# Local attention of a 12-layer transformer stack: probabilities divided before they are turned, outputs produced turned

## The reference, cut to what matters

```python
def local_attention(q, k, v):               # 16 heads, 64 features a head, windows of 32 tokens
    ...                                     # each window looks at the one before it and at itself
    sim = jnp.einsum('bhwie,bhwje->bhwij', bq, bk2) * QK_SCALE
    sim = jnp.where(mask, -jnp.finfo(sim.dtype).max, sim)
    attn = jax.nn.softmax(sim, -1)
    out = jnp.einsum('bhwij,bhwje->bhwie', attn, bv2)
    return out.reshape(b, h, n, d)

def attn_layer(x, Wqkv, qs, ksc, Wo):
    ...                                     # q, k, v from x; q and k to length 1, scaled, rotated
    out = local_attention(q, k, v)
    out = out.transpose(0, 2, 1, 3).reshape(b, n, INNER)
    return out @ Wo
```

## Time and profile before

| what | us |
|---|---|
| median of 3 runs | 4365.75 |
| lowest and highest run | 4363.63 and 4371.05 |
| span of the profiled execution | 4366.1 |
| busy TensorE, matmuls (weight loads) | 3908.6 (2744.4) |
| busy GpSimd | 3002.4 |
| busy VectorE | 2756.9 |
| busy ScalarE | 2682.7 |

### The profile page before, as it was taken

The page is one execution under the profiler, slowest core; times in us unless marked ns, Lnnn a source line. Parts: engine busy times, 40 slices in busy tenths (PEclk is TensorE's granted clock), DMA queues, the critical chain, the costliest instruction groups (busy, mean ns, idle before and its releaser), DMA issues.

```text
span 4366.1 us, 169503 instructions
## 1 busy us (share of the span) xinstructions
PE 3908.6 (90%) x69444; PEld 2744.4 (63%) x69444; DVE 2756.9 (63%) x4939; ACT 2682.7 (61%) x5560; POOL 3002.4 (69%) x1858
## 2 busy tenths in 40 slices
PE   7889999999999999977999999999999998265975
PEld 5556666676666766744766666666666665153645
DVE  5566666676766666734667676677676764623751
ACT  5657666676666767644676666767666675133752
POOL 0088888888888888814988888888888884611011
PEclk9999999999999999979999999999999998577987
DMA  2033433434334344311344343443433432031004
GB/s 68 2 86 90 112 97 95 110 93 107 97 95 104 96 105 102 93 46 42 96 102 104 92 111 93 103 108 92 108 98 96 108 92 55 0 104 27 2 13 127
DMA packets 349837, 367.90 MB, mean 84 GB/s; under 512 B 58738, under 2 KB 285299, under 8 KB 348787
## 3 DMA queue, kind: packets, MB, share of 16 engines
q1 hardware_dynamic: 338834, 348.59, 31.4%
q0 software_dynamic: 2048, 4.20, 0.3%
q10 hardware_dynamic: 8160, 3.93, 0.3%
HBM read 246.79 MB, written 109.71 MB: 82 GB/s over the span
## 4 chain that ended last, share of the span: by engine, by line
PE 38%; DVE 4%; ACT 4%; issue 3%; POOL 2%; DMA 1%; DVEq 0%; POOLq 0%; ACTq 0%
PE banks L328 6%; PE banks L356 4%; PE banks L369 4%; PE banks L416 3%; PE banks L460 3%; PE banks L312 2%; PE banks L295 2%; PE banks L401 2%; PE banks L454 1%; PE banks L386 1%; PE banks L1382 1%; ACT arena L996 1%; PE banks L1402 1%; DVE arena L619 1%; PE banks L923 1%
## 5 line engine op out<-in xcount | busy, mean ns | idle before, releaser
L690 POOL TENSOR_TENSOR arena<-arena 128x512 f32<-128x512 f32 x768 | 959.6, 1270 | 414.6 <-DVE arena L619 235.2
L695 POOL TENSOR_TENSOR arena<-arena 128x1024 f32<-128x1024 f32 x384 | 906.0, 2359 | 30.1
L692 POOL TENSOR_TENSOR arena<-arena 128x1024 f32<-128x1024 f32 x384 | 907.5, 2363 | 0.0
L619 DVE SCALAR_TENSOR_TENSOR arena<-arena,banks 128x512 f32<-128x512 f32 x768 | 493.5, 684 | 503.8 <-ACT arena L502 500.9
L328 PE MATMUL banks<-w_qk,arena 128*128 128x512 f32 x1536 | 734.5, 601 | 16.0 <-DVE arena L719 10.6
L470 ACT COPY arena<-banks 128x512 f32<-128x512 f32 x384 | 224.3, 584 | 656.8 <-PE banks L416 656.7
L612 DVE TENSOR_REDUCE arena<-arena 128x8 f32<-128x512 f32 x768 | 494.0, 679 | 86.1 <-ACT arena L486 84.2
L486 ACT ACTIVATE arena<-banks 128x512 f32<-128x512 f32 x768 | 441.3, 593 | 62.5 <-PE banks L328 50.5
L416 PE MATMUL banks<-ident,arena 128*128 128x128 f32 x3072 | 425.3, 282 | 28.6 <-POOL arena L695 20.5
L328 PEld LDWEIGHTS banks<-w_qk,arena 128*128 128x128 f32 x1536 | 276.4, 193 | 271.4 <-issue 271.4
L586 DVE TENSOR_REDUCE arena<-banks 128x8 f32<-128x512 f32 x384 | 264.0, 687 | 212.5 <-PE banks L312 212.1
(11 more groups left out here) (217 smaller groups left out, 6519.4 us busy)
## 6 DMA issues: line engine op xcount, KB each, us to landing
v_rows<-arena SPq DMA_DIRECT2D x1536, 64.0 KB
arena<-v_rows SPq DMA_DIRECT2D x768, 128.0 KB
arena<-v_rows SPq DMA_DIRECT2D x768, 112.0 KB
arena<-in_moe_w SPq DMA_DIRECT2D x30, 515.5 KB, 3.8
w_qk<-in_stack_qk SPq DMA_DIRECT2D x48, 256.0 KB, 3.0
w_v<-in_stack_v SPq DMA_DIRECT2D x48, 128.0 KB, 3.3
w_o<-in_stack_o SPq DMA_DIRECT2D x12, 512.0 KB, 3.9
w_w<-in_stack_w SPq DMA_DIRECT2D x12, 341.0 KB, 3.1
```

Source lines behind the costliest of these rows:

```text
L619: last = nc.vector.scalar_tensor_tensor(qn[:, :, tile], rn, 1e12, bank(M, tile).rearrange("p (h q d) -> p h q d", h=GH, q=2), ALU.min, ALU ...
L690: nc.gpsimd.tensor_tensor(f.sined[:, :, :, half, :], x[:, :, :, 1 - half, :], sines[:, :, mine].unsqueeze(1).to_broadcast([D, GH, 4, DH // ...
L692: nc.gpsimd.tensor_tensor(rot, x.rearrange("p h t a d -> p h t (a d)"), cosines.unsqueeze(1).to_broadcast([D, GH, 4, DH]), ALU.mult).then_ ...
L695: nc.gpsimd.tensor_tensor(rot, rot, f.sined.rearrange("p h t a d -> p h t (a d)"), ALU.add).then_inc(S.rotated, 1)
```

## The change

VectorE multiplies the probabilities `p` (128 by 512, in SBUF) by the reciprocal of their sums in place, right behind the reciprocal. TensorE turns the probabilities when that is done (`normed`) instead of when the exponential is done. In the output products the operands swap places: the weights are the 64 by 64 values of a window, the moving operand 32 columns of turned probabilities, and a product is 64 features by 32 tokens. With that the outputs need neither the multiplication of line 596 nor the turn of line 386; ScalarE copies them from the banks into `ot` directly, and the rows of the output weights are laid out to match. The outputs now use columns 0 to 255 of banks 4 and 5, as the scores do: they wait until the scores of this step have been shifted into `zs`, and the next scores wait until they have been copied. Their place in TensorE's order moves from behind the scores to behind the projection of queries and keys. On ScalarE their copy stands ahead of the copy of the values in all steps. VectorE no longer waits for outputs before the maximum. The buffer `o` and the signal `outs_turned` go.

```diff
 def pe_stack_step(M, st):
...
         st.wait(S.shifted, u)
-
-        st.wait(S.normed, u - 1)
+        st.wait(S.outs_taken, u - 1)
...
-    if st.on(4):
-        u = s - 4
-        st.wait(S.probs_taken, u + 1)
-        pe.wait_ge(S.v_loaded, st.n64 + 64 * (u + 1))
-        st.wait(S.normed, u)
-        pe.sem_inc(M.s.pe_waited)
-        for hp in range(2):
-            for win in range(NW):
-                c = 32 * (win % 4)
-                o = T + (win // 4 * 2 + hp) * DH
-                for par in range(2):
-                    r = slice(64 * par, 64 * par + 64)
-                    last = pe.matmul(bank(M, 4 + par)[c:c + 32, o:o + DH], f.pt[r, win // 4, hp, c:c + 32],
-                                     f.vb[r, u % 2, win, hp, :], start=True, stop=True)
-        last.then_inc(S.outs, 1)
...
-    if s % G == 3:
-
-
-        pe_stack_outs_turned(M, st)
-        pe_stack_probs_turned(M, st)
-        pe_stack_values(M, st)
-    else:
-        pe_stack_values(M, st)
+    pe_stack_outs(M, st)
+    pe_stack_values(M, st)
+    if s % G != 3:
         pe_stack_hidden(M, st, 1)
-        pe_stack_probs_turned(M, st)
-        pe_stack_outs_turned(M, st)
+    pe_stack_probs_turned(M, st)
...
+def pe_stack_outs(M, st):
+
+
+    pe, s, S, f = st.eng, st.s, M.st, stack_buffers(M)
+    if st.on(4):
+        u = s - 4
+        st.wait(S.probs_taken, u + 1)
+        pe.wait_ge(S.v_loaded, st.n64 + 64 * (u + 1))
+
+        if st.on(3):
+            st.wait(S.shifted, u + 2)
+        st.wait(S.outs_taken, u)
+        pe.sem_inc(M.s.pe_waited)
+        for win in range(NW):
+            c = 32 * (win % 4)
+            for hp in range(2):
+                for par in range(2):
+                    r = slice(64 * par, 64 * par + 64)
+                    last = pe.matmul(bank(M, 4 + par)[64 * hp:64 * hp + 64, 32 * win:32 * win + 32],
+                                     f.vb[r, u % 2, win, hp, :], f.pt[r, win // 4, hp, c:c + 32],
+                                     start=True, stop=True)
+        last.then_inc(S.outs, 1)
...
 def pe_stack_probs_turned(M, st):
...
-        st.wait(S.probs, u + 1)
+        st.wait(S.normed, u + 1)
...
 def pe_stack_heads(M, st, qk):
...
-        st.wait(S.outs_taken, u - 2)
+        st.wait(S.heads_taken, u)
...
 def act_stack_step(M, st):
...
-    if s % G == 3:
-        act_stack_outs(M, st)
-        act_stack_probs(M, st)
-        act_stack_values(M, st)
-    else:
-        act_stack_values(M, st)
+    act_stack_outs(M, st)
+    act_stack_values(M, st)
+    if s % G != 3:
         act_stack_hidden(M, st, 1)
-        act_stack_probs(M, st)
+    act_stack_probs(M, st)
...
     if s % G == 3:
         act_stack_hidden(M, st, 1)
-    else:
-        act_stack_outs(M, st)
     act_stack_hidden(M, st, 2)
...
 def act_stack_outs(M, st):
...
-        st.wait(S.outs_turned, u + 1)
+        st.wait(S.outs, u + 1)
...
-        nc.scalar.copy(stack_hidden(M).ot[:, u % G].rearrange("p h t -> p (h t)"), bank(M, 3)).then_inc(S.outs_taken, 1)
+        nc.scalar.copy(stack_hidden(M).ot[:, u % G], M.ps[:, 4:6, 0:T]).then_inc(S.outs_taken, 1)
...
 def dve_stack_step(M, st):
...
-        st.wait(S.outs, u)
...
-    if st.on(4):
-        u = s - 4
-        st.wait(S.outs, u + 1)
-        st.wait(S.inverted, u + 1)
-        st.wait(S.outs_turned, u)
-        nc.vector.tensor_tensor(f.o.rearrange("p (x b) d -> p x b d", b=2), two_banks(M, T, DH),
-                                f.inv.rearrange("p (x b) -> p x b", b=2).unsqueeze(3).to_broadcast([D, 4, 2, DH]),
-                                ALU.mult).then_inc(S.normed, 1)
-    if st.on(3):
-        u = s - 3
         st.wait(S.probs, u + 1)
         nc.vector.tensor_reduce(f.total, f.p, AX.X, ALU.add).then_inc(S.summed, 1)
         st.wait(S.summed, u + 1)
-        st.wait(S.normed, u)
         nc.vector.reciprocal(f.inv, f.total).then_inc(S.inverted, 1)
+        st.wait(S.inverted, u + 1)
+        nc.vector.tensor_tensor(f.p, f.p, f.inv.unsqueeze(2).to_broadcast([D, 8, KW]), ALU.mult).then_inc(S.normed, 1)
```

## The result

| | before | after |
|---|---|---|
| median | 4364.69 us (4363.57 to 4371.05, 4 runs) | 4773.74 us (4765.19 to 4780.62, 4 runs) |
| ratio | 1 | 1.0932, 95% interval 1.0914 to 1.0949 |
| span of the profiled execution | 4366.1 us | 4777.0 us |

The changed kernel is 9.3% slower, 409 us. The prediction said 4798 us and 4480 to 4900.

What follows compares the result with a forecast made beforehand. TensorE was taken as full (97% busy), closely followed by a loop through X, VectorE and GpSimd. Eight steps came to 76.5 against 67.5 us; 48 x 9.0 = 432 us on 4366.1 gave 4798 us, range 4480 to 4900.

Steps and rivals of the forecast that it cites:

- the rival with waits at any phase: Multiplication asks anywhere in GpSimd's time: mean wait 0.8 us instead of 2.1, total 4606; shares 0.70 with the main forecast.
- X: End of the scaling of queries and keys on VectorE, which frees VectorE, banks and GpSimd's rotation; 2.05 us into the next step.
- the hold: VectorE's multiplication, both operands in SBUF, waits for GpSimd's running instruction, up to 2.4 us, then takes 0.55; chance 0.70 (4600 to 4900).
- A bare step: Step without extras, from X to next X: multiplication ends at 5.75, turn starts at 5.8, plus 3.02, giving 8.82 us.
- The extras: Additions to eight steps of 8.82 us: feed-forward +0.69 and +0.74, last feed-forward matmul +1.0, steps behind a projection +1.6 and +1.9.
- by TensorE's own order: After the first step ending with the projection, TensorE's sequence alone sets 10.4 us from turn to turn, +1.6.
- its sister: The second step ending with the projection: VectorE asks at about X + 5.1 to 5.5, costing +1.5 or +2.4, taken as 1.9.
- The output block: The 64 output passes on TensorE, moved behind the projection of queries and keys: 1.1 us, ends 0.87 and 1.5.
- TensorE's own sum: TensorE's change per step from removed turn, new output passes and their old place: -0.1 us, ends -0.3 and +0.3.
- the rival of 5300: Weight loads queue on TensorE: output passes take 3.65 us, eight steps some 20 us longer; 0.07 together with half clock.
- The rival without a hold: Multiplication takes 0.69 us, loop 6.9, about 1 us extra in each of four steps: 71 per eight, 4534; chance 0.10.
- The rival of half clock: New waits of up to 2 us lower TensorE's granted clock, doubling matmuls at 1.2 GHz: above 4900; 0.07 together with queued loads.

## Why the prediction was right, step by step

- **The multiplication is held by GpSimd and ends 0.55 us behind it.** As forecast: mean 2.14 us in the range of 2 to 2.7, tail 0.55, most of them (286 of 384) in the third instruction, so the rival with waits at any phase (4606) did not come. In six of eight steps it asked at X + 2.98 to 3.74 (forecast 3.10 and 3.84) and ended at X + 5.43 to 5.84 (forecast 5.75). The kernel with the reciprocals in a bank shows that the hold is the cause.
- **GpSimd pays too.** "Some 0.5 longer" was too much: the fourth instruction took 2.69 instead of 2.36, 0.33 more. I had scaled from the earlier trace rows, where a multiplication of 1024 columns made it about 1 us longer.
- **A bare step of 8.82 us.** Steps 3, 6 and 7 took 8.54, 8.68 and 8.85 from turn to turn. Right.
- **The extras.** Forecast were 1.0 for the matmul ahead of the turn, 0.69 and 0.74 for two feed-forward instructions on VectorE, and 1.6 and 1.9 for the two steps behind a projection. Over 8.82, row 2 has 1.48, in which both the matmul (1.0) and the late X of step 1 (0.74) were to show; rows 4 and 0 have 2.21 each. The step that I let come "by TensorE's own order" (10.4) is held as well: its multiplication asks at X + 5.26 to 5.48 and falls into GpSimd's fourth instruction, ending at X + 8.02, near the other end (2.4) of what I weighed for its sister. So a wait that I had put down to TensorE alone was a hold. Against this, the feed-forward instruction of step 1 shows as 0.6 in its X, and that of step 5 as nothing (row 6 has 8.68); row 5 has 0.4 that I did not forecast, since the turn starts 0.55 behind the multiplication there. The errors cancelled: 76.4 against 76.5. The total is better than its terms, and that part is luck.
- **The output block.** Taken as 1.1 with ends at 0.87 and 1.5. It is 1.07 from start to start (1083.41 to 1084.48), and its neighbours grew: the projection ahead of it from 1.72 to 1.81 and the values behind it from 0.86 to 0.97 (medians over all steps), 1.27 in all. TensorE's own sum is thus about +0.1 a step instead of -0.1. Loads that queue, the rival of 5300, are refuted.
- **The order.** The prediction had X "3.02 us after the turn starts", by ScalarE's copy, and gave the hold the whole of the loss. Both stand in the same loop, and the experiments split them: without the hold 209 us go, without the hold and the tie 381. The rival without a hold was put at 4534 and the run gave 4564, 30 us off. As charged, four steps are longer there, s = 1, 3, 5 and 6, by 1.26, 0.89, 1.26 and 0.75 us; the other four are within 0.1 us of before, where I had taken off 0.1 us a step for TensorE.
- **TensorE's busy share.** Forecast down to about 80%, measured 90% in the stretch. Here my own sums did not agree: 65.5 us of busy time in 67.4 before, less 0.8, over 76.5 would have been 85%. For the other 5 points I have an argument only: a group's busy time includes its last matmul's tail, which lay over the next group before and now lies in a hole.
- **The clock.** TensorE's waits for the multiplication, up to 3.0 us long, left the granted clock at 0.99 in the stretch. The rival of half clock did not come.
- **The profiled execution.** Span 4777.0 less 4366.1 is 411 us; the loop's 430 less that leaves 19. Most of it is found at the starts of layers, for which the prediction took nothing off: the first step s = 7 after each of the ten starts inside the modules loses 1.4 to 3.2 us less than that step's median.

What is left of the change without hold and tie, the 56 us between the two kernels with the moved logarithm, is in the main a wait of TensorE for the feed-forward pieces. Their waits (idle before the matmuls: total, times, longest), with the new outputs:

```profile
PE banks L417 <- ACT ln_sq L528: 30.2, 48, 1.4
...
PE banks L445 <- ACT xc L542: 20.6, 52, 0.8
PE banks L445 <- DVE ln_sq L621: 13.4, 19, 1.6
```

and with the outputs of before:

```profile
PE banks L460 <- DVE ln_sq L651: 5.0, 4, 1.6
PE banks L460 <- ACT xc L563: 4.7, 6, 0.8
...
PE banks L432 <- ACT ln_sq L549: 2.9, 2, 1.4
```

64 us against 13: heads and pieces come 0.75 us earlier in the step, since the outputs no longer stand ahead of them, and their data do not. These rows are not a full account. In the old place the outputs wait too:

```profile
PE banks L312 <- ACT arena L524: 14.0, 47, 0.4
```

And a wait under the tail of the group before is not idle time. Start to start it is seen in full. The steps are 0.4 us longer in s = 1, 5 and 6 and within 0.1 elsewhere. In these three, heads to the piece behind them take 1.14, 1.70 and 1.13 us with the new outputs, against 0.93, 1.14 and 0.93. In s = 6 the last piece starts 0.94 us behind the turn of the probabilities in both kernels, so the time of the turn that went is waited out. Against this, the way from scores to outputs held waits of about 0.2 us in s = 5 and 0.4 in s = 6 in the old order, which the new one does not have. The prediction has this loss in its rival without a hold, as heads and projection that come too early; the pieces of the feed-forward part it did not name. That another place for these pieces would end it was not tried.

## What to carry to other kernels

Before an elementwise step is moved on VectorE, see where its operands lie and what GpSimd is running at that moment: two SBUF operands under a long GpSimd instruction cost the wait to its end (the instruction became three times as long here), and moving even the small operand into a bank took that away. A step that loses its slack to a new dependence is worked out as a loop, from one end of the late engine's work to the next, and every path in the loop is listed: of two paths of equal length, cutting one alone brings little (44 us for the tie); cutting what stands in both, the hold, brought 209, and both together 381, more than the sum. An engine that is 97% busy can still be waiting at its seams; an order on another engine gave the old kernel 34 us.

## What the runs showed of the hardware that was not expected

- The hold works the same whichever instruction holds. In the changed kernel 368 multiplications started 0.15 us or more before the end of a GpSimd instruction, and all ended 0.545 to 0.554 us behind that end, 0.14 less than the length alone. The four that started 0.06 to 0.09 us before it took their 0.69 us, and so did 48 products of the kernel with the extra product that started 0.05 to 0.11 us before it (0.68 us). So the first 0.14 us of the instruction run beside GpSimd.
- GpSimd's loss is of another size than VectorE's: the fourth instruction behind a held multiplication of 512 columns is 0.33 us longer (2.69 against 2.36). It starts 0.08 us behind the end of the third in the steps shown, when the multiplication still has 0.47 to run.
- The 64 output passes with 64-column weights and 32 moving columns in four tiles have starts 14.5 ns apart (0.916 us for 63 gaps); the 64 passes with 32-column weights and 64 moving columns in eight tiles, before, 10.0 ns (0.633 us). The pace follows neither the moving columns, which halve, nor the loaded columns, which double: it grows by 1.45.
